# Building the adjacency counts of a graph network: narrower node ranges for the second and third run of edges, and attribute halves made for six and five windows at once

## The reference

```python
x = _layernorm(x + _L0_gnn_ref(x, src, dst))                    # 10 hops of normalised neighbour sums
x = _layernorm(x + _L1_gnn_ref(x, edge_index, edge_attr_32, We, be, W1, b1, gamma, beta, W2, b2))
x = _layernorm(x + _L2_gnn_ref(x, W, b, Wr, br, src, dst))      # 2 hops
x = _layernorm(x + _L3_gnn_ref(x, edge_index, W, att_src, att_dst, bias))  # attention, 4 heads

# in each of them, with seg = dst:
agg = jax.ops.segment_sum(h[src], dst, num_segments=n)
# in the second:
msg = x[src] + (edge_attr @ We + be)
```

## Time and profile before

| | |
|---|---|
| median of 3 runs | 1373.35 us (1371.07 to 1373.67) |
| the profiled execution | 1373.54 us |
| its span, first to last instruction | 1371.7 us |
| busy in the span: TensorE matmuls, weight loads | 1188.4 us, 1119.0 us |
| VectorE, ScalarE, GpSimd | 884.5 us, 634.3 us, 63.2 us |
| granted TensorE clock, mean over the span | 0.907 |
| line 923, `ohk` | 352 instructions, 122.9 us |
| line 925, `ohp` | 88 instructions, 77.6 us |
| line 668, eviction into `C` | 242 instructions, 111.2 us |
| the chain that ended last, by engine | PE 62%, DVE 26%, issue 5%, ACT 4% |

### The profile page before, as it was taken

The page is one execution under the profiler, slowest core; times in us unless marked ns, Lnnn a source line. Parts: engine busy times, 40 slices in busy tenths (PEclk is TensorE's granted clock), DMA queues, the critical chain, the costliest instruction groups (busy, mean ns, idle before and its releaser), DMA issues.

```text
span 1371.7 us, 41245 instructions
## 1 busy us (share of the span) xinstructions
PE 1188.4 (87%) x16976; PEld 1119.0 (82%) x16976; DVE 884.5 (64%) x2403; ACT 634.3 (46%) x1250; POOL 63.2 (5%) x113
## 2 busy tenths in 40 slices
PE   0688778886989999899999599689989989998997
PEld 0578777786989999899988499579978978997996
DVE  1999999984334424344561633677777877777786
ACT  0676666660000000000011201478777878787886
POOL 2000000000111101111000011100000000000000
PEclk9867876766999999999999599799999999999999
DMA  1544444411000000000000000000000000000000
GB/s 29 79 64 66 61 64 67 61 24 25 3 3 2 3 3 2 3 2 3 3 2 2 1 2 3 2 1 2 1 2 2 1 2 2 2 2 1 6 12 11
DMA packets 136693, 21.52 MB, mean 16 GB/s; under 512 B 136088, under 2 KB 136505, under 8 KB 136537
## 3 DMA queue, kind: packets, MB, share of 16 engines
q1 hardware_dynamic: 135188, 18.73, 9.1%
q10 hardware_dynamic: 1252, 0.31, 0.1%
q0 software_dynamic: 96, 0.16, 0.0%
HBM read 18.39 MB, written 0.80 MB: 14 GB/s over the span
## 4 chain that ended last, share of the span: by engine, by line
PE 62%; DVE 26%; issue 5%; ACT 4%; DMA 1%; SPq 0%; DVEq 0%; POOL 0%; ACTq 0%; POOLq 0%
PE bank L1607 33%; PE bank L1732 16%; PE bank L1728 9%; DVE ohk L923 7%; DVE ohp L925 4%; DVE raw L913 2%; DVE Mr L1388 2%; ACT Mr L834 2%; ACT F L797 1%; DVE F L1297 1%; DVE eaT L1289 1%; PE bank L1723 1%; PE bank L1538 1%; DVE xs L1150 1%; DVE ohj L883 1%
## 5 line engine op out<-in xcount | busy, mean ns | idle before, releaser
L1607 PE MATMUL bank<-GH,C 128*128 128x128 f16 x8125 | 467.4, 221 | 30.7 <-DVE GH L1051 23.4
L1607 PEld LDWEIGHTS bank<-GH,C 128*128 128x128 f16 x8125 | 464.4, 99 | 36.0 <-DVE GH L1051 22.6
L1732 PE MATMUL bank<-F,Mr 128*128 128x260 f16 (+1 forms) x2538 | 365.3, 274 | 11.8 <-DVE Mr L1388 8.8
L834 ACT ACTIVATE Mr<-eaT,steep 128x640 f16<-128x640 f32 x433 | 325.8, 822 | 36.4 <-PE bank L1732 35.7
L1388 DVE TENSOR_TENSOR Mr<-Mr,C 128x640 f16<-128x640 f16 x433 | 199.1, 487 | 100.4 <-ACT Mr L834 98.7
L1732 PEld LDWEIGHTS bank<-F,Mr 128*128 128x128 f16 x2538 | 225.8, 98 | 36.3 <-DVE Mr L1388 8.1
L1728 PE MATMUL bank<-FN,C 128*128 128x130 f16 x2500 | 232.6, 221 | 0.3 <-DVE r L1306 0.3
L708 ACT ACTIVATE plo<-bank 128x256 f32<-128x256 f32 (+1 forms) x91 | 32.8, 360 | 427.6 <-PE bank L1607 427.6
L1068 DVE TENSOR_TENSOR S<-bank,plo 128x256 f32<-128x256 f32 (+1 forms) x91 | 35.9, 394 | 275.1 <-ACT plo L708 275.1
L1728 PEld LDWEIGHTS bank<-FN,C 128*128 128x128 f16 x2500 | 186.2, 98 | 13.6 <-DVE r L1306 0.8
L1523 PE MATMUL bank<-ohk,ohp 128*128 128x100 f16 (+3 forms) x1210 | 158.2, 280 | 10.5 <-ACT C L668 6.5
(11 more groups left out here) (222 smaller groups left out, 877.6 us busy)
## 6 DMA issues: line engine op xcount, KB each, us to landing
raw<-in_edges_dram SPq DMA_DIRECT2D x242, 68.0 KB, 2.1
xs<-in_x_dram SPq DMA_DIRECT2D x1, 768.0 KB
out_dram<-xs SPq DMA_DIRECT2D x4, 160.0 KB
wg<-in_L_gnn_W_dram ACTq DMA_DIRECT2D x2, 64.0 KB
z<-in_L_gnn_att_src_dram SPq DMA_DIRECT2D x1, 128.0 KB
z<-in_L_gnn_att_dst_dram SPq DMA_DIRECT2D x1, 128.0 KB
out_dram<-xs SPq DMA_DIRECT2D x1, 128.0 KB
wts<-in_L_gnn_W_dram ACTq DMA_DIRECT2D x3, 16.0 KB
```

Source lines behind the costliest of these rows:

```text
L834: act.activation(Mr[:, mi % RB, :], nadS, ACT.Sigmoid, bias=steep[:, h, t:t + 1], scale=-STEEP / XS).then_inc(s_step, 1)
L1607: last = pe.matmul(bank[:, b, jj * 2 * D:(jj + 1) * 2 * D], C[:, t, (t0 + jj) * P:(t0 + jj + 1) * P], GH[:, par, t, :], start=t == 0 and j ...
L1732: return pe.matmul(bank[:, k, a_:z_], Mr[:, mi % RB, j * P:(j + 1) * P], F[:, t, a_:z_], start=start, stop=t == T - 1)
```

## The change

Two things are edited. First, `NODES`: the second run of edges is allowed the targets 2 to 10 instead of 2 to 12, the third 6 to 12 instead of 5 to 12. The one-hot `ohk` of a window shrinks from 726 to 652 columns. To cover a window's 13 targets exactly, `PART` now has six matmuls instead of five; their columns add up to 650 instead of 725. The attribute matmuls at line 1527 shrink from 11 and 8 columns to 9 and 7.

Second, the attribute pieces are the two `HALVES` (six and five windows) instead of the four `UNITS`, on all three engines that handle them, and they move within the group. `high_attrs` for the next group stands behind evictions 5 and 10 (before: 2, 5, 8 and 10), `low_attrs` for the next group's first half behind eviction 9 (before: 6 and 9), for the own second half behind eviction 0 (before: 0 and 3). On VectorE the own second half's remainder follows unit 0 (before: units 0 and 1), the next group's first half's follows unit 3 (before: units 2 and 3). The counts in the waits are adapted.

```diff
--- before.py
+++ after.py
@@ -69,8 +69,8 @@
     SEED = float(0x5F3759DF)
     RING = 3
     SLOTS = 2
-    PART = ((0, 0, 6), (1, 2, 6), (1, 6, 13), (2, 5, 13), (3, 9, 13))
-    NODES = ((0, 6), (2, 13), (5, 13), (9, 13))
+    PART = ((0, 0, 6), (1, 2, 6), (1, 6, 11), (2, 6, 11), (2, 11, 13), (3, 9, 13))
+    NODES = ((0, 6), (2, 11), (6, 13), (9, 13))
     WIDE = [(T * (b_ - a_) + 1) // 2 * 2 for a_, b_ in NODES]
     OK = [sum(WIDE[:k]) for k in range(K + 1)]
     UNITS = ((0, 3), (3, 6), (6, 9), (9, WG))
@@ -451,7 +451,7 @@
                     g = i * 2 + (2 + par)
                     for half in range(2):
 
-                        sp.wait_ge(s_lo, i * (2 * NU) + (par * NU + 2 * half + 2))
+                        sp.wait_ge(s_lo, i * 4 + (par * 2 + half + 1))
                         load_half(g, par, half)
 
             sp.wait_ge(s_degacc, 1)
@@ -652,14 +652,14 @@
 
             def high_attrs(i, k, u):
 
-                w0, w1_ = UNITS[u]
+                w0, w1_ = HALVES[u]
                 act.wait_ge(s_raw[k % 2], i * (16 * WG) + 16 * WG * (k // 2 + 1))
                 act.activation(eahl[:, w0 * K:w1_ * K, 0:DE], attrs(k % 2, w0, w1_), ACT.Copy).then_inc(s_hi, 1)
 
             def low_attrs(i, k, u):
 
-                w0, w1_ = UNITS[u]
-                act.wait_ge(s_dif, i * (2 * NU) + (k * NU + u + 1))
+                w0, w1_ = HALVES[u]
+                act.wait_ge(s_dif, i * 4 + (k * 2 + u + 1))
                 act.activation(eahl[:, w0 * K:w1_ * K, DE:2 * DE], attrs(k % 2, w0, w1_), ACT.Copy, scale=LO).then_inc(s_lo, 1)
 
             def evict(i, par, w):
@@ -670,21 +670,20 @@
             def build_group(i, par, more):
                 for w in range(WG):
                     evict(i, par, w)
-                    if w in (0, 3):
-                        low_attrs(i, par, 2 + w // 3)
-                    if more and w in (6, 9):
-                        low_attrs(i, par + 1, w // 3 - 2)
-                    if more and w + 1 in [u_[1] for u_ in UNITS]:
-                        high_attrs(i, par + 1, [u_[1] for u_ in UNITS].index(w + 1))
+                    if w == 0:
+                        low_attrs(i, par, 1)
+                    if more and w == 9:
+                        low_attrs(i, par + 1, 0)
+                    if more and w in (5, 10):
+                        high_attrs(i, par + 1, w // 10)
                     if more and w == 4:
                         positions(i, par + 1)
                 act.activation(eaT[0:S1, bass.ds((i * 2 + par) * (WG * W), WG * W)], pea[par][0:65, 0:WG * W], ACT.Copy).then_inc(s_eaev, 1)
 
             positions(0, 0)
-            for u in range(NU):
+            for u in range(2):
                 high_attrs(0, 0, u)
-            for u in range(2):
-                low_attrs(0, 0, u)
+            low_attrs(0, 0, 0)
             with act.Fori(0, G // 2 - 1) as i:
                 for par in range(2):
                     build_group(i, par, True)
@@ -908,8 +907,8 @@
 
             def rest(i, k, u):
 
-                w0, w1_ = UNITS[u]
-                v.wait_ge(s_hi, i * (2 * NU) + (k * NU + u + 1))
+                w0, w1_ = HALVES[u]
+                v.wait_ge(s_hi, i * 4 + (k * 2 + u + 1))
                 v.tensor_tensor(attrs(k % 2, w0, w1_), attrs(k % 2, w0, w1_), eahl[:, w0 * K:w1_ * K, 0:DE], ALU.subtract).then_inc(s_dif, 1)
 
             def build_unit(i, par, u):
@@ -929,18 +928,17 @@
                 v.wait_ge(s_pl, i * 4 + (2 * par + 2))
                 for u in range(NU):
                     build_unit(i, par, u)
-                    if u < 2:
-                        rest(i, par, u + 2)
-                    elif more:
-                        rest(i, par + 1, u - 2)
+                    if u == 0:
+                        rest(i, par, 1)
+                    elif more and u == 3:
+                        rest(i, par + 1, 0)
                     if more and u:
                         keys(i, par + 1, u - 1)
 
             for step in range(3):
                 keys(0, 0, step)
             c.here()
-            for u in range(2):
-                rest(0, 0, u)
+            rest(0, 0, 0)
             with v.Fori(0, G // 2 - 1) as i:
                 c.loop(i, 2 * 4)
                 for par in range(2):
@@ -1513,7 +1511,7 @@
                         o = w % (SLOTS * U)
                         if w in [u_[0] for u_ in UNITS]:
                             u = [u_[0] for u_ in UNITS].index(w)
-                            pe.wait_ge(s_lo, g * NU + (u + 1))
+                            pe.wait_ge(s_lo, g * 2 + (1 + (u >= 2)))
                             pe.wait_ge(s_oh, g * NU + (u + 1))
                         pe.wait_ge(s_evict, wi + (1 + AGO - back(w)))
                         if w == 0:
```

## The result

The changed kernel takes 1361.07 us (median of four runs, 1359.95 to 1362.61) against 1373.51; the ratio is 0.9907, with a 95% interval of 0.9895 to 0.9919. The profiled execution took 1361.0 us with a span of 1359.2, so 12.5 us of the span have to be found.

The account below looks back on a forecast made before the run. VectorE was taken to bound the adjacency build. The terms -8.9 - 2.9 + 1.0 + 1.8 - 0.4 made -9.4 us from 1373.54, written as 1364.0 us, with a gain range of 6 to 12.2 us.

Parts of the forecast that it names:

- (a): VectorE's `ohk` in the build: 74 fewer columns per window from narrower node ranges, -8.9 us over 21 periods.
- (b): VectorE's attribute remainders in the build: two per group instead of four save the fixed part, -2.9 us.
- (c): TensorE's window in the build: VectorE's wait before unit 2 grows to a mean 0.08 to 0.10 us, +1.0 us.
- the lower bound of the text: TensorE's sixth matmul and weight-load pair costs nothing, because its load and columns hide in the stream.
- the outer case of the text: TensorE's window of 14 pairs at the skill page's 81 ns each: 1.13 us, the kernel near 1390 us.
- (d): Handover through ScalarE in the build: VectorE waits at line 912 in about 8 groups, +1.8 us.
- middle bound: Wait in the ScalarE handover if the net change of TensorE's window is zero: 4.4 us.
- rival 2: ScalarE handover in the build: slow TensorE clock makes VectorE wait, 1380.2 us; chance 0.06 slower, 0.01 same.
- under 3 us in all: Sign at line 912: VectorE's idle before it stays under 3 us; reaching 8 us would show the forecast wrong.
- (e): Hidden or small effects, including the prologue and the last group of the build: -0.4 us.
- Rival 4: After the build: gain given back behind the load of `x` or by the hops' clock, about 1373 us; chance 0.07.
- Rival 1: TensorE's sixth pair in the build is paid in full: gain only 4.0 us, 1369.5 us; chance 0.12.

Follow-up runs that it names:

- late remainder: Changed kernel with VectorE's five-window remainder moved behind unit 1 and ScalarE's low part for it behind eviction 3: 1352.08 us, ratio 0.9850.
- the padded kernel: Kernel before with 22 matmuls (44 instructions) added in a never-taken TensorE branch ahead of the hop loop: 1364.99 us, ratio 0.9920.
- the changed kernel padded by 106: Changed kernel with 106 matmuls (212 instructions) added in a never-taken TensorE branch ahead of the hop loop: 1373.09 us, ratio 0.9990.

## Why the prediction was right or wrong

**(a) narrower ranges, -8.9: right.** `ohk` of 678 elements was announced at about 500 ns and takes 510:

```profile
L922 DVE TENSOR_TENSOR ohk<-iota_key,key 128x678 f16<-128x678 f16 x55 | 28.0, 510 | 0.0
...
L912 DVE TENSOR_TENSOR raw<-raw,eahl 128x768 f32<-128x768 f32 x19 | 18.3, 961 | 0.0
...
L912 DVE TENSOR_TENSOR raw<-raw,eahl 128x640 f32<-128x640 f32 x18 | 14.9, 826 | 7.0 <-ACT eahl L657 7.0
```

Alone it brought the period from 12.01 to 11.55: 9.6 us over 21 periods, the wait at unit 2 included.

**(b) two remainders for four, -2.9: right in the build, once nothing waits.** 961 and 826 ns against 950 and 820 announced. From the narrower ranges alone (11.55) to the late remainder (11.39) is 3.5 us of build, of which the total times show nothing beyond their scatter.

**(c) the wait at unit 2, +1.0: slightly too dear.** The sixth pair costs nothing, the lower bound of the text, and the idle in front of unit 2 is gone (0.37 us from the keys to unit 2, 175.92 to 176.29). A window of 14 pairs in 1.13 us, the outer case of the text, is ruled out by the 0.89.

**(d) the handover through ScalarE, +1.8: the step that failed in the build.** The chain was drawn right, down to the line number and the order of ScalarE's work, but it was sized by the clock of the old trace. I took 8 of 22 groups as late at window 9, because in 13 TensorE arrived early. In the changed kernel 94% of the windows, told by their length, run at 1.2 GHz, where it was 59%, and nearly every group is late: 18 waits of 0.41 us between 60 and 290 us. The difference between the changed kernel and the late remainder is the price: 9.8 us over 21 periods (11.85 against 11.39), five times my term and above the 4.4 I had as its middle bound. This is the mechanism of rival 2, with faster windows than it assumed (0.89, not 0.96): it ate three quarters of the 13.1 us of (a) and (b), not more. I had given it 0.07. The idle before line 912 came to 7.3 us in this stretch and to 8.4 over the whole build, where "under 3 us in all" was announced and 8 was named as the sign of being wrong. The sign I predicted for the build holds, but by itself the build would have moved the kernel by 3.7 us.

**(e) -0.4: right in size.** The first unit 0 is ready 0.2 us earlier, where 0.1 later was expected, and the stretch from the last group's unit 0 to the end of the build is 0.15 shorter.

That the slow level fills more of the stage goes with the narrower one-hots: about 60 to 73% of the windows in the seven kernels with 725 columns, about 75 to 86% in the four with 650 in which VectorE does not wait, and 94 to 98% in the three in which it does. Why is not shown.

**What was missing: the instruction stream.** This is the larger failure. The sum had no term for anything behind the build: it treated the edit as if it ended there. Rival 4 named "another clock pattern in the hops" only as a way to lose. Yet the trace before had the row: a timeline of TensorE over the hops shows one matmul, a stall of 2.1 to 2.8 us marked "issue", and then 1249. And the list of TensorE's instructions showed that 40 more would stand ahead. Neither was put beside the other. It is worth 7.3 us of stalls plus the slower matmuls behind them, 8.8 us of median as the padded kernel measures it.

**The sum.** 9.4 forecast against 12.5, of which 3.7 from the build. The forecast number came close by luck: a build 5.7 us dearer than forecast, and some 9 us from a place it didn't look at. (Rival 1's sum of -4.0 also left out the -0.4 of (e).)

## What to carry to other kernels

When an edit changes how many instructions stand ahead of a long loop, look at how the loop's turns begin in the trace: a few instructions, then a stall with "issue" as its reason, was a block boundary behind the jump here, and instructions in a branch that is never taken move it. To judge an edit in such a kernel, hold that offset the same on both sides, or the stage that was not touched decides the comparison.

A piece of work that is made coarser moves its deadline as well as its cost: put the larger piece where its producer is done at the *slow* level of the producer's clock, not at the mean of the trace. Here one unit later was worth 8 to 9 us.

And take the halves of a change apart before keeping it: here one half alone was as good as any mended form of both.

## What was not expected of the hardware

- TensorE's position in the instruction stream is worth 9 to 13 us in 1373 here, with a period of 256 instructions and a sharp edge: offsets 240, 252, -4 and 0 stall, 12 to 128 do not.
- The stall is what is left of some 6 us: with it TensorE goes on that long after a pass's end, whatever the number of matmuls ahead of the stop; without it, after 3.0 to 3.6 us.
- The clock adds to it, but less regularly: behind the long pauses a pass's matmuls took 71.7 to 72.4 us (eight passes), behind the short ones 71.5 to 71.6 in fifteen passes and 69.96 in five.
- At 1.2 GHz a change of a window's time follows its columns: 75 columns fewer are 0.062 us, two matmuls and weight loads fewer are 0.00.
- The granted clock of a stretch can mislead: in the changed kernel padded by 106 it is 0.76 over 60 to 280 us, with 97% of the windows at the length of the slow level; without the padding 0.54, with 94%. The lengths of the windows were the surer reading.
